# Plain attention: the two kinds of score matmul alternate in PE's list, and the exponentials' scores run seven banks ahead instead of eight

## What is computed

```python
q = q.reshape(B, S, H, DK); k = ...; v = ...        # B=2, S=2048, H=16, DK=16
scores = jnp.einsum('bqhd,bkhd->bhqk', q, k) / np.sqrt(DK)
attn = jax.nn.softmax(scores, axis=-1)
o = jnp.einsum('bhqk,bkhd->bqhd', attn, v)
```

## Time and profile before

| | |
|---|---|
| median of 3 runs | 4429.42 us (4396.91 to 4430.73) |
| the profiled execution | 4403.5 us, of which the span from the first to the last instruction is 4401.8 us |
| TensorE clock granted, mean over the span | 0.943 |
| PE busy | 91% |
| DVE busy | 79% |
| ACT busy | 68% |
| plain attention, first `s` to last copy | about 2275 to 3675 us of the span |

### The profile page before, as it was taken

The page is one execution under the profiler, slowest core; times in us unless marked ns, Lnnn a source line. Parts: engine busy times, 40 slices in busy tenths (PEclk is TensorE's granted clock), DMA queues, the critical chain, the costliest instruction groups (busy, mean ns, idle before and its releaser), DMA issues. The chain is left out here.

```text
span 4401.8 us, 77253 instructions
## 1 busy us (share of the span) xinstructions
PE 3988.2 (91%) x26592; PEld 2101.9 (48%) x26592; DVE 3491.7 (79%) x6304; ACT 2990.7 (68%) x5821; POOL 1447.8 (33%) x1405
## 2 busy tenths in 40 slices
PE   8699999999999999996879999999999996689997
PEld 5344444444444444443533333333333333589997
DVE  6788888888888888853778889888989882577775
ACT  3077777777778777783228888888888883256664
POOL 0356666666566666652000000000000000623222
PEclk9599999999999999998969999999999997699998
DMA  8567666666566666654653323323232303676664
GB/s 311 146 159 165 160 162 158 168 162 162 143 166 163 163 150 168 161 119 136 237 108 44 46 41 44 55 30 55 37 48 41 45 11 72 177 212 176 171 174 112
DMA packets 486195, 556.39 MB, mean 126 GB/s; under 512 B 60260, under 2 KB 426836, under 8 KB 476524
## 3 DMA queue, kind: packets, MB, share of 16 engines
q1 hardware_dynamic: 465980, 526.94, 49.2%
q0 software_dynamic: 19824, 24.52, 3.5%
HBM read 347.67 MB, written 206.76 MB: 126 GB/s over the span
## 5 line engine op out<-in xcount | busy, mean ns | idle before, releaser
L1098 ACT ACTIVATE ra_p<-ra_psS 128x512 f32<-128x512 f32 x2048 | 1089.7, 605 | 360.1 <-PE ra_psS L1175 262.7
L371 DVE TENSOR_REDUCE pa_pm<-pa_psA 128x2 f32<-128x1024 f32 x1024 | 1208.4, 1219 | 134.7 <-PE pa_psA L460 134.7
L1009 DVE TENSOR_REDUCE ra_pm<-ra_psA 128x1 f32<-128x896 f32 x1024 | 1113.7, 1088 | 195.3 <-PE ra_psA L1133 181.8
L434 ACT ACTIVATE pa_p<-pa_psS 128x512 f32<-128x512 f32 x2048 | 1063.5, 603 | 247.5 <-PE pa_psS L486 243.3
L486 PE MATMUL pa_psS<-pa_qs,pa_zs 50*128 50x512 f32 x2048 | 793.0, 464 | 77.9 <-ACT pa_p L434 63.2
L460 PE MATMUL pa_psA<-pa_zs,pa_qs 48*128 48x512 f32 x2048 | 796.7, 472 | 38.0 <-DMA pa_zs<-k_halves 17.8
L1133 PE MATMUL ra_psA<-ra_zs,ra_qs 48*128 48x512 f32 x2048 | 732.6, 453 | 43.0 <-DVE ra_pm L1011 22.0
L1175 PE MATMUL ra_psS<-ra_qs,ra_zs 50*128 50x512 f32 (+3 forms) x2176 | 711.4, 410 | 32.8 <-ACT ra_p L1098 19.4
L486 PEld LDWEIGHTS pa_psS<-pa_qs,pa_zs 50*128 50x128 f32 x2048 | 342.1, 185 | 626.5 <-ACT pa_p L434 608.0
L1206 PE MATMUL ra_psO<-ra_p,ra_vs 128*32 128x512 f32 (+3 forms) x6400 | 563.7, 457 | 0.0
L497 PE MATMUL pa_psO<-pa_p,pa_vs 128*32 128x512 f32 x4096 | 547.2, 606 | 0.0
(11 more groups left out here) (247 smaller groups left out, 4970.0 us busy)
## 6 DMA issues: line engine op xcount, KB each, us to landing
relative_rows<-ra_rst SPq DMA_DIRECT2D x128, 512.0 KB, 3.9
ra_blk<-window_rows SPq DMA_DIRECT2D x128, 512.0 KB
mo_w_raw<-ffn_W SPq DMA_DIRECT2D x58, 1024.0 KB, 5.5
ra_zs<-k_halves SPq DMA_DIRECT2D x192, 248.0 KB, 7.4
ra_dl<-relative_rows SPq DMA_DIRECT2D x128, 256.0 KB, 5.4
window_rows<-ra_pc SPq DMA_DIRECT2D x128, 256.0 KB
pa_qs<-q_halves SPq DMA_DIRECT2D x192, 128.0 KB, 6.4
pa_zs<-k_halves SPq DMA_DIRECT2D x192, 128.0 KB, 7.0
```

Source lines behind the costliest of these rows:

```text
L371: dve.reduce_max(pm[:, par, 2 * a:2 * a + 2], psA[w][:, :, :], AX.X).then_inc(s_am.h, 1)
L434: act.activation(pr[:, i % NPR, :], psS[:, slot(i), :], ACT.Exp).then_inc(s_ex.h, 1)
L1009: dve.reduce_max(pm[:, q, i, 2 * left:2 * left + 1], psA[w][:, lo:lo + 2 * G - P], AX.X).then_inc(s_far.h, 1)
L1098: act.activation(dst, psS[:, slot(i), :], ACT.Exp if kind == "E" else ACT.Copy).then_inc(s_cp.h, 1)
```

## The change

Two constants differ; all lists, semaphores and counts follow from them.

```diff
-LEAD = 8
+LEAD = 7
 EVAC = 22
 ...
-ORDER = "assaOsaas"
+ORDER = "asasOassa"
```

## The result

The changed kernel takes 4422.09 us (median of 20 runs, 4404.14 to 4454.38) against 4407.62 us for the kernel before (20 runs, 4381.02 to 4430.73). The medians are 14.5 us apart; the ratio of the two groups of runs is 1.0039, with a 95% interval of 1.0021 to 1.0058: some 17 us slower, between 9 and 26. That is no change by the prediction's bound of 1%, and slower once it is measured often enough. The forecast was +5.7 us: the right side, a third of the size.

What follows compares the result with a forecast made beforehand. Bound: a 2.61 us loop between ACT's exponentials and PE's `s` and O. M turn with its copy +14.0, change of heads -7.7, other copies -1.0, ends +0.4: +5.7 us, 4435 on the median of three runs; range 4396 to 4450.

Steps and rivals of the forecast that it cites:

- The loop: First exponential, `s` of pair 4, O, `s` of pair 1, back to the exponential: 2.61 us a cycle, unchanged.
- Rival C: Lone `s` in pair 4 gets its weights early: 0.09 us less in each of 512 cycles, 4389 us; chance 0.05.
- Rival D: In the first pair after O, `s` starts a full matmul behind `a`: 0.23 us a cycle, 4553 us; chance 0.06.
- B: Rival: the wait for DVE behind the M turn costs nothing, the change of heads still gains: 4412 to 4421; chance 0.14.
- the M turn: Behind DVE's three reductions, the `s` of pair 1 now waits behind an `a` for DVE: +0.36 us, 31 times.
- E: Rival: nothing visible, as pairs start together and the M wait and heads' wait cancel: 4429 us; chance 0.05.
- The change of heads: Between heads, bank 63 comes a pair later and the wait shrinks from +0.49 to +0.25: -0.25 us, 31 times.
- The copy of `psO`: ACT's copy moves behind the first exponential and delays O by 0.09 instead of 0.10 us: -0.01, 96 times; +0.09, 31 times.
- The lag in the pairs: In pair 1 `s` is now second, behind `a`: taken as 0, at most +0.01 us for each of 512 cycles.

Runs made afterwards that it cites:

- e3: The kernel before with the changed kernel's order within the pairs alone, eight banks ahead as before: 44.03 us a head, 4412.86 us.
- e5: The kernel before with only the two pairs behind O ordered as in the changed kernel: 44.05 us a head, 4403.17 us.
- e2: The kernel before with `LEAD` 7 instead of 8 alone, old order, `EVAC` 22: 43.64 us a head, 4413.47 us.
- e4: The kernel before with `LEAD` 7 and `EVAC` 21, old order, copy of `psO` where it was: 43.33 us a head, 4396.85 us.
- e7: The kernel before with the three `psS` banks used in turn through all heads: 43.10 us a head, 4386.97 us.
- e1: The changed kernel with `EVAC` 21 instead of 22, so the copy of `psO` precedes the first exponential behind O: 43.75 us a head, 4403.59 us.
- e6: The changed kernel with PE's wait for the copy of `psO` placed ahead of its wait for the exponentials: 43.77 us a head, 4408.21 us.
- e8: The kernel before with banks in turn, `LEAD` 7, `EVAC` 22 and PE's two waits swapped, old order: 43.05 us a head, 4389.26 us.

## Why the prediction was right in direction and short in size

**The loop** stayed as worked out: O 0.43 behind a lone `s`, ordinary cycles within 0.01 of 2.61. Rival C (weights of the lone `s` loaded early) fell: that load still starts with its wait's end, at 3018.43, idle 0.31, ended by ACT. The rule of the Trainium skill that stood behind it, page "TensorE: Matmul & The Clock Gate", section "What happens when you issue a matmul", does not carry over to a LDWEIGHTS with an open wait; a load without one does start while matmuls are in flight (17.34, its matmul at 17.58). Rival D fell too: `a` first directly behind O, the `s` starts 0.01 later. B fell with the M turn, which is paid, and E with the measured 17 us.

**The M turn** was forecast at +0.36 and measured at +0.39 (3.21 against 2.82). The mechanism is shown by e3 and e5. DVE's end, which was to stay where it was, moved by 0.02: it is 2.62 behind the start of the group before (3003.71 to 3006.33), and was 2.60 (3010.55 to 3013.15).

**The change of heads** was forecast at -0.25 and measured at -0.25 (2.85 against 3.10), shown by e2 and e4, and from the other side by e7.

**The copy of `psO`** is the term that was mis-sized. The step read: the copy "ends at 1.65, and the next O, which waits for it, can start at 1.70 instead of 1.61: +0.09". The copy does end there, at 1.63 (17.23 to 18.86). But the step took the 0.05 between an exponential's end and the `s` behind it as the price of any wait of PE. O has two waits in a row, the late one second, and that one is an instruction of its own; the matmul starts 0.145 behind the copy, at 1.78, and the cycle is 2.767, +0.155. Four of them instead of three times 0.10 are +0.32 a head, where the sum had +0.06. The bound given for it (0.2 each) did hold it.

**The lag in the pairs** was set at 0, with 0.01 a cycle as the bound. It measured 0.005 to 0.007 in ordinary cycles. e3 and e5 show it (2.616), e2 and e4 do not (2.610), so it belongs to the pairs behind O; that it is the `a` ahead of the `s` in the first of them is argued. Of a head it is small and not well resolved: kernels that differ in the order alone (e3 and before, e1 and e4, changed and e2) are 0.44, 0.42 and 0.50 apart, which less the M turn's 0.39 leaves 0.03 to 0.11.

Together 0.39 - 0.25 + 0.32 = 0.46 of the measured 0.55 us a head, and the 0.09 left is no more than the lag can be; 31 heads of 0.55 are 17 us, as the stage (+17.5) and the ratio (+17) have it. With the copy as forecast and no lag it would have been 0.20 a head, 6 us.

The time, 4422, lies in the range, but 13 us under the 4435 named, and that it came so near is luck: the sum was put on a median of three runs that turned out 22 us higher than that of twenty, and the change was put 11 us too low. The range, set wide for the difference between runs, would have held either error alone. That difference goes with TensorE's granted clock over the whole run: among the changed kernel's twenty, 4404.14 us goes with 0.945 and 4454.38 with 0.932. In the profiled executions, whose clock runs from 0.938 to 0.946 over the whole run, the plain attention stands at 1.00 (0.997 in e2), so the clock falls in other stages; what makes it fall, and whether it is the cause of the longer time or goes along with it, stays open.

## What to carry to other kernels

Where two engines feed each other through a few buffers and neither is full, write the cycle as a chain of starts, and check every edit against that chain alone: the large idle times elsewhere did not matter, and the 0.06 us that were missing in the price of a copy on the chain came back 127 times. A constant that counts ahead (`LEAD`) moves everything that is counted against it (`EVAC`); move both, or price the shift. Put the instruction that may wait for the slower partner behind, not ahead of, the one on the chain, and of two waits of PE in a row put the one that comes last in time first in the list, as e6 did.

## What the runs showed of the hardware

PE's start behind a released wait depends on where that wait stands. As the only or the first one it is carried by the weight load: 0.05 us from the end of ACT's instruction to the load, and the matmul with it. As the second of two, of which the first was long met, it is an instruction of PE's sequencer ahead of the load, 0.051 us long: 0.11 us to the load and 0.145 to the matmul (the changed kernel and e2), and 0.05 again once swapped (e6, e8), where that instruction is over 0.39 us before the copy ends. The Trainium skill, page "Perfetto Trace Analysis", section "Identifying Dependency Chains", says that an instruction that waits on several engines may have separate instructions with the additional waits ahead of it; the trace agrees and shows them as EVENT_SEMAPHORE. The page gives no price; here it is 0.06 us to the load and 0.09 us a cycle.
